# Attention scores as 64-row matmuls, one half of TensorE's array per head of a pair

## The reference

```
scores = einsum('bhqd,bhkd->bhqk', q, k) / sqrt(8) + mask   # mask: alibi + causal
attn   = softmax(scores);  out = attn @ v @ Wo + bo;  x = x + out;  x = x + ffn(layer_norm(x))
```

## Time and profile before

| | |
|---|---|
| median of 3 runs | 1680.35 us (1676.8 to 1682.39) |
| profiled execution, first to last instruction | 1676.2 us; the page has no other time for it |
| TensorE busy | 1460.0 us, 87% |
| VectorE busy | 1131.6 us, 68% |
| ScalarE busy | 1004.2 us, 60% |
| chain that ended last | PE 62%, issue 15%, DVE 13%, ACT 6% |
| mean granted TensorE clock | 0.963 of full speed |

### The profile page before, as it was taken

How to read it: one execution, slowest core, us unless ns; L and a number is a source line. 1 busy time by engine, 2 the same in 40 slices (tenths; PEclk the granted TensorE clock), 3 DMA queues, 4 the chain that set the end, 5 groups by cost and what they waited for, 6 DMA issues and landing times.

```text
span 1676.2 us, 33128 instructions
## 1 busy us (share of the span) xinstructions
PE 1460.0 (87%) x9729; PEld 717.1 (43%) x9888; DVE 1131.6 (68%) x3539; ACT 1004.2 (60%) x1214; POOL 226.7 (14%) x400
## 2 busy tenths in 40 slices
PE   3689898999889998899988999799988999899984
PEld 2334343454435444353444544344443534344343
DVE  5667667776676765767677766577668666677725
ACT  2045775667666675567756676565756677566741
POOL 6001200121011300113001210013001120010001
PEclk8579999999999999999999999899999999999997
DMA  5101212112120301212121021201212121201010
GB/s 184 51 20 39 93 30 76 48 28 93 31 71 27 96 29 31 81 31 93 31 58 42 28 93 31 84 29 43 93 28 59 31 93 31 74 28 30 4 46 13
DMA packets 83691, 88.87 MB, mean 53 GB/s; under 512 B 9896, under 2 KB 76976, under 8 KB 83504
## 3 DMA queue, kind: packets, MB, share of 16 engines
q1 hardware_dynamic: 83504, 86.60, 17.4%
HBM read 54.32 MB, written 33.55 MB: 52 GB/s over the span
## 4 chain that ended last, share of the span: by engine, by line
PE 62%; issue 15%; DVE 13%; ACT 6%; DMA 1%; POOL 1%; DVEq 1%; SPq 0%; ACTq 0%; POOLq 0%
PE PS L755 14%; PE PS L730 13%; PE PS L692 11%; PE PS L741 9%; PE PS L683 8%; DVE PS L978 4%; DVE mx L982 2%; PE PS L713 2%; PE PS L744 2%; ACT PR L578 2%; DVE mx L978 2%; DVE acc L910 1%; ACT hb L560 1%; PE PS L717 1%; PE PS L661 1%
## 5 line engine op out<-in xcount | busy, mean ns | idle before, releaser
L578 ACT ACTIVATE PR<-PS 128x1024 f32<-128x1024 f32 (+3 forms) x768 | 612.2, 809 | 517.8 <-PE PS L744 313.9
L978 DVE CUSTOM_DVE_ANT_0 PS<-PS,mkw 128x128 f32<-128x128 f32 (+3 forms) x1024 | 502.9, 499 | 305.4 <-PE PS L730 286.7
L730 PE MATMUL PS<-Kop,Qop 128*128 128x128 bf16 (+2 forms) x1406 | 435.3, 334 | 98.9 <-DVE mx L978 64.3
L741 PE MATMUL PS<-Qop,Kop 128*128 128x512 bf16 (+3 forms) x1507 | 402.1, 329 | 40.5 <-ACT PR L578 17.5
L730 PEld LDWEIGHTS PS<-Kop,Qop 128*128 128x128 bf16 x1536 | 148.4, 98 | 576.7 <-DVE mx L978 278.2
L982 DVE TENSOR_REDUCE mx<-PS 128x1 f32<-128x512 f32 x512 | 351.4, 686 | 51.7 <-PE PS L730 48.8
L755 PE MATMUL PS<-PR,vbuf 128*32 128x512 f32 (+3 forms) x3072 | 331.2, 503 | 0.5 <-ACT PR L578 0.4
L744 PE MATMUL PS<-idb,mk 128*128 128x128 bf16 x1024 | 206.1, 222 | 1.5 <-DMA Qop<-mrow 1.0
L692 PE MATMUL PS<-wE,hb 128*128 128x128 f32 x1536 | 198.3, 280 | 9.4 <-ACT xnT L541 3.8
L692 PEld LDWEIGHTS PS<-wE,hb 128*128 128x128 f32 x1536 | 185.5, 193 | 26.8 <-ACT xnT L541 7.3
L741 PEld LDWEIGHTS PS<-Qop,Kop 128*128 128x128 bf16 x1536 | 150.8, 98 | 94.5 <-ACT PR L578 28.2
(11 more groups left out here) (77 smaller groups left out, 942.4 us busy)
## 6 DMA issues: line engine op xcount, KB each, us to landing
Qop<-qst SPq DMA_DIRECT2D x128, 128.0 KB, 2.8
Kop<-kst SPq DMA_DIRECT2D x64, 256.0 KB, 3.1
kst<-parts SPq DMA_DIRECT2D x32, 256.0 KB, 3.0
qst<-parts SPq DMA_DIRECT2D x16, 384.0 KB, 2.8
wE<-in_moe SPq DMA_DIRECT2D x8, 514.0 KB, 4.1
kst<-parts SPq DMA_DIRECT2D x32, 128.0 KB, 2.8
qst<-parts SPq DMA_DIRECT2D x16, 256.0 KB, 2.9
Qop<-mrow SPq DMA_DIRECT2D x256, 3.0 KB
```

The lines of the kernel that those rows point to most:

```text
L578: act.activation(PR[:, c % 4, :, 0:n], PS[:, 2 * (c % 2):2 * (c % 2) + 2, 0:n], ACT.Exp)\
L730: pe.matmul(PS[:, 5 + k % 2, 0:n], Qop[:, par, h % 2, h // 2, P * i:P * i + P], Kop[:, kb, h // 2, k0:k0 + n], start=True, stop=True).then ...
L741: last = pe.matmul(bank[:, 0:n], Kop[:, kb, a, P * kt:P * kt + P], Qop[:, par, j, a, q0:q0 + n], start=True, stop=not DIAG[t])
L978: dve.tensor_tensor_reduce(chunk, chunk, mkw[:, 512 - n:512], 1.0, -3.0e38, ALU.add, ALU.max, mx[:, par, i, h, c:c + 1]).then_inc(S["s_p1m ...
```

## The change

1. Both score passes slice their operands to the 64 rows of one head (`r`). `Qop` loses its zero halves and the dimension that held them: it is `Qop[:, par, a, :]`, laid out as `Kop` is. A head's score matmul uses rows 0 to 63 or 64 to 127 of the array, over all 128 columns.
2. In `p2_pair` the two score matmuls come first, then the two mask matmuls, which stay at 128 rows.
3. `P1_CHUNKS` runs over heads innermost. So chunk k uses the lower half of the array for even k and the upper for odd k, and for query tiles 4 to 7 (slots 8 to 23) the four full chunks come before the four that end on the diagonal.
4. The zeroing of `Qop` at the start goes, and SP's wait for it. Each unit's load of `Qop` is one DMA for all 128 partitions in place of two; the semaphore counts follow.

```diff
 P1_CHUNKS = [(i, h, c, 512 * c, min(512, P * (i + 1) - 512 * c))
-             for i in range(TB) for h in range(G) for c in range(1 + i // 4)]
+             for i in range(TB) for c in range(1 + i // 4) for h in range(G)]
...
-        Qop = sb("Qop", [P, 2, 2, 2, T], BF16)
+        Qop = sb("Qop", [P, 2, 2, T], BF16)
...
-                for j in range(2):
-                    r = slice(ROWS * j, ROWS * j + ROWS)
-                    sp.dma_start(Qop[r, par, j, :, cols], qun[u, r, :, cols]).then_inc(c, 16)
+                sp.dma_start(Qop[:, par, :, cols], qun[u, :, :, cols]).then_inc(c, 16)
                 sp.dma_start(Kop[:, kb, :, cols], kun[u, :, :, cols]).then_inc(c, 16)
...
-            pool.memset(Qop[:, :, :, :, :], 0.0).then_inc(S["s_ms"], 1)
-            pool.wait_ge(S["s_ms"], 4)
+            pool.wait_ge(S["s_ms"], 3)
...
-                pe.matmul(PS[:, 5 + k % 2, 0:n], Qop[:, par, h % 2, h // 2, P * i:P * i + P],
-                          Kop[:, kb, h // 2, k0:k0 + n], start=True, stop=True).then_inc(S["s_p1"], 1)
+                r = slice(ROWS * (h % 2), ROWS * (h % 2) + ROWS)
+                pe.matmul(PS[:, 5 + k % 2, 0:n], Qop[r, par, h // 2, P * i:P * i + P],
+                          Kop[r, kb, h // 2, k0:k0 + n], start=True, stop=True).then_inc(S["s_p1"], 1)
...
                 for j in range(2):
-                    bank = PS[:, 2 * (c % 2) + j, :]
-                    last = pe.matmul(bank[:, 0:n], Kop[:, kb, a, P * kt:P * kt + P], Qop[:, par, j, a, q0:q0 + n],
-                                     start=True, stop=not DIAG[t])
-                    if DIAG[t]:
-                        last = pe.matmul(bank[:, 0:P], mk2[:, :], idb[:, :], start=False, stop=True)
+                    r = slice(ROWS * j, ROWS * j + ROWS)
+                    last = pe.matmul(PS[:, 2 * (c % 2) + j, 0:n], Kop[r, kb, a, P * kt:P * kt + P],
+                                     Qop[r, par, a, q0:q0 + n], start=True, stop=not DIAG[t])
+                if DIAG[t]:
+                    for j in range(2):
+                        last = pe.matmul(PS[:, 2 * (c % 2) + j, 0:P], mk2[:, :], idb[:, :], start=False, stop=True)
                 last.then_inc(S["s_s2"], 1)
```

More of the change, by code:

```diff
@@ L302, in _ @@
             sp.wait_ge(S["c_con"], 64)
-            sp.wait_ge(S["s_ms"], 4)
             def load(u, par, kb, half):
@@ L329, in minus_max @@
                     r = ROWS * (h % 2) + 8 * 3 + 7
-                    sp.dma_start(Qop[r:r + 17:8, par, h % 2, h // 2, cols], mrow[3 * h:3 * h + 3, par, cols])\
+                    sp.dma_start(Qop[r:r + 17:8, par, h // 2, cols], mrow[3 * h:3 * h + 3, par, cols])\
                         .then_inc(c_m[par][half], 16)
@@ L724, in p1_chunk @@
                 if k == 0:
-                    pe.wait_ge(c_ldl[par], 48 * (nth + 1))
+                    pe.wait_ge(c_ldl[par], 32 * (nth + 1))
                 if k == P1L:
-                    pe.wait_ge(c_ldr[par], 48 * (nth + 1))
+                    pe.wait_ge(c_ldr[par], 32 * (nth + 1))
                 if k >= 2 or not first:
                     pe.wait_ge(S["s_p1m"], P1N * U + k - 1)
-                pe.matmul(PS[:, 5 + k % 2, 0:n], Qop[:, par, h % 2, h // 2, P * i:P * i + P],
-                          Kop[:, kb, h // 2, k0:k0 + n], start=True, stop=True).then_inc(S["s_p1"], 1)
+                r = slice(ROWS * (h % 2), ROWS * (h % 2) + ROWS)
+                pe.matmul(PS[:, 5 + k % 2, 0:n], Qop[r, par, h // 2, P * i:P * i + P],
+                          Kop[r, kb, h // 2, k0:k0 + n], start=True, stop=True).then_inc(S["s_p1"], 1)
             def p2_pair(U, par, kb, nth, c):
@@ L1082, in _ @@
             dve.tensor_tensor(gate[:, :, :], eq[:, 0, :, :], eq[:, 1, :, :], ALU.add).then_inc(S["s_gate"], 1)
-            dve.wait_ge(S["s_ms"], 4)
+            dve.wait_ge(S["s_ms"], 3)
             for k in range(P1N):
```

## The result

The changed kernel takes **1699.19 us** (median of 3 runs, 1697.25 to 1705.68) against 1680.35 us. The ratio is 1.0131, with a 95% interval of 1.0107 to 1.0155: 19 us slower by the medians, 22 by the ratio (18 to 26 by its interval). The forecast was 1683 us, "within 0.3%". The time lies inside the range of 1645 to 1714, on the slower side (chance 0.40), but outside the 1670 to 1692 of the likeliest case.

A forecast was written before the change was run, and what follows sets the result against it. TensorE was taken to bound the kernel, with 62% of the chain. The terms -75 + 6 + 60 + 17 - 10 + 6 - 1 = +3 us on the 1680.35 us median gave 1683 us, range 1645 to 1714.

The forecast's parts named there:

- likeliest case: The whole kernel: the sum of all terms holds, 1683 us, with its own range 1670 to 1692, chance 0.52.
- Pair overlap: Second pass: a pair's two 64-row score matmuls overlap fully, saving half of their 151 us on the chain, -75 us.
- no overlap: Rival, second pass's pair: 64-row matmuls go one after the other, +82 us, 1762 us, chance 0.08.
- in part: Rival, second pass's pair: it saves a third of its time, not half, 25 us higher, 1708 us, chance 0.05.
- The maxima's cap: Even slots of 16 to 23 without filler: maxima limit the pair's saving to 0.11 of 0.22 us, +6 us.
- Changes of shape: Between 64-row scores and 128-row masks or fillers: each change costs 0.10 us, +60 us at masks, +17 us at fillers.
- Neighbouring chunks: First pass: a second chunk and the next slot's first chunk could overlap in different halves, -10 us, bounds 0 and -60.
- Order of chunks: Slots 8 and 9: four full chunks in a row make slot 9's second chunk start later, +6 us, upper bound +19.
- Start: Kernel start: without the zeroing of Qop the first rstd comes about a microsecond earlier, -1 us.
- The time around the span: Outside the profiled span of 1676.2 us, against the median 1680.35: 4 us that the change doesn't touch.
- the clock: Rival: half an array in use or shorter pairs lower TensorE's clock within units, near 1775 us or 1714, chance 0.07.
- if the granted clock falls within the units: One of three signs, read in the profile after, that would show the prediction wrong; the clock's row was to stay 0.96 to 0.97.

The follow-up runs named there:

- e4: The kernel before with only the first pass's score matmuls in 64 rows, the pairs still 128-row, old order of chunks: 1742.48 us, ratio 1.0380.
- e1: The kernel before, all score matmuls of 128 rows, with only the new order of chunks: 1677.79 us, ratio 0.9991.
- e5: The changed kernel with two useless 128-row matmuls added in each of slots 16 and 17, first units of phases 2 to 8: 1689.26 us, ratio 1.0053.
- e7: The changed kernel with two useless 64-row matmuls added in each of slots 16 and 17, first units of phases 2 to 8: 1689.12 us, ratio 1.0056.
- e2: The changed kernel with the old order of chunks: 1695.97 us, ratio 1.0103.
- e10: The kernel before with 64-row score matmuls in all of slots 16 to 23, with or without fillers, both passes: 1683.04 us, ratio 1.0029.
- e8: The kernel before with 64-row score matmuls only in slot pairs from 16 on without masks or fillers, both passes: 1675.14 us, ratio 0.9969.
- e9: The changed kernel with the old order of chunks and two useless matmuls in each of slots 16 and 17 of those first units: 1689.92 us, ratio 1.0064.
- e3: The kernel before with only the second pass's pairs in 64 rows, masks behind both score matmuls, first pass still 128-row: 1699.15 us, ratio 1.0125.

## Why the prediction was off, step by step

- **Pair overlap, -75.** The mechanism was right, and stronger than stated, since the first pass's chunks take part. By the chain L738 lost 66 us. The rivals "no overlap" and "in part" are ruled out. So is the estimate by the Trainium skill's factor ("TensorE: Matmul & The Clock Gate", Part 3, 3.07 for four row tiles, from which I had 1.54 for two): two halves run here at twice the rate of one.
- **The maxima's cap, +6**, was too small. It was worked out for slots of 512 columns without filler alone, from one gap of 0.11 us. The two passes now finish 0.43 us earlier in such a slot, and the next line of the timeline is a wait of 0.78 us for the maximum. This waiting is what matters below.
- **Changes of shape, +60 and +17.** The size, 0.10 us, measured 0.094 each way. The share on the path, taken as 0.6, measured 0.46 where e4 isolates it (a lower value than the pure share, since neighbouring chunks overlap there): by this share an estimate of 1312 x 0.46 x 0.094 = 57 us in place of 77.
- **Neighbouring chunks, -10.** They overlap, but behind the maxima; not separated from the pair's overlap by any run.
- **Order of chunks, +6.** e1 shows no effect (ratio 0.9991 of 1680 us: -1.5 us, interval -4 to +1). Slots 8 and 9 do wait as predicted (`796.80` in the rows below, a chunk held up by the maximum), for 0.4 to 0.5 us in half the units, and slots 10, 11, 20 and 21 give most of it back.
- **Start, -1.** 1.2 us.
- **The time around the span.** The prediction read 4 us (1680.35 less 1676.2). In each later run the device time is about 1.8 us above its own span; the rest was the difference between two runs. The forecast starts from the median, so it doesn't move.

The timeline of slots 8 and 9 after, for the order of chunks:

```profile
795.85 0.38 PE L738 MATMUL PS<-Qop,Kop 64*128 64x512 bf16 x2
...
796.05 1.89 DVE L980 TENSOR_REDUCE mx<-PS 128x1 f32<-128x512 f32 x3 [0.82 <-PE PS L727]
...
796.80 0.39 PE L727 MATMUL PS<-Kop,Qop 64*128 64x512 bf16 x1 [0.35 <-DVE mx L980]
```

The balance of these terms came out close to the forecast of +3: the 24 units that don't open a phase are 6 us longer, and with the clock held in slots 16 to 18 (e5) the first units of phases 2 to 8 are 0.6 us longer together. In part that is luck. The pair comes to -66 by the chain and the changes of shape to +57 by the share of e4, together 11 us below their -75 and +77. No run measures the terms of the maxima and the neighbouring chunks apart; a cap larger than +6 would close the gap, which isn't shown. That 1699 lies inside the range is owed to its width: the time came from a rival that was priced at 1714 to 1775. By the prediction's own sign of being wrong ("if the granted clock falls within the units") it was wrong in its mechanism.

**The step that failed is the clock.** The prediction wrote "the clock's row stays between 0.96 and 0.97" and gave a fall within the units a chance of 0.07. The row is 0.952, half-clock time in the units went from 24 to 61 us, and 9 of the 19 us (by the ratios, 13 of 22) come back when TensorE is kept busy in seven places. The rival named "half an array in use, or shorter pairs". The argument against it, that "fillers and V matmuls use 128 rows in nearly every slot pair", answers only the first, and e7 speaks against the first too. The second, shorter work and so more idle time, is what the runs bear out. What I should have asked is how long TensorE will now stand idle where DVE sets the pace: the earlier trace rows had shown that a stretch of this kernel with little for TensorE ran at half the clock. The numbers of the rival were worked out too high as well (1775, or 1714 for a third): the falls cover 37 us more of the units, not 150 or 50.

What stays open: why the falls take other phases in nearly the same program (after, e2 and e10 differ), why e5, e7, e8, e9 and e10 have a fall in the second unit of the last phase and after, e2 and before have none, and the 4 us in the first unit, which was not tried.

## What to carry to other kernels

When a change makes TensorE faster in a stretch where another engine sets the pace, work out how long TensorE will idle there, and look in the trace where the granted clock already falls and how little TensorE did ahead of it. Here the long fp32 work behind such a stretch cost more than the stretch had saved (`h` 2.00 us in place of 0.86). A few useless matmuls are a cheap test of this, and the same on the kernel before is its control. Packing two half-height matmuls paid here where it added no change of shape (e8, 0.3%); each change costs 0.09 us, a little less than the columns of a 256-column matmul (0.11), so groups of one shape should be made as long as the order allows.

## What the runs showed of the hardware

- Two matmuls in different row halves run fully at once: four of 512 columns took 0.23 us to the start of the last and 0.22 for its columns, 0.45 us, in place of 0.66 and 0.22. The first chunk and the pair's matmul in the other half start within 0.01 us (822.96), and the second chunk starts beside the pair's other matmul.
- Matmuls in different halves can start out of the program's order. The first chunk and the pair's first matmul lie in the lower half, the pair's second matmul in the upper, and it carries the increment of the pair's semaphore. In 248 of the 256 pairs without masks of the kernel after, the trace has that one start first. In e3, where the chunk ahead takes all rows, it does so in none of 256. The increment stayed safe to wait for: where ACT waited for it, ACT began no less than 0.42 us after the later start, the same as where both start together.
- A change between 64 and 128 rows costs 0.094 us each way (93 ns in, 96 out), the same as between 128 and 32 columns.
- Ahead of the falls shown here (after and e8) TensorE had idled more than the kernel before did in the same slots; two 512-column matmuls in each of two slots kept the clock at 1.00 in slots 16 to 18 (5.67 us in e5 and in e7), in 64 rows as in 128.
